# Three half-precision products instead of one fp32 product for the queries of layer 0

## What is computed

```python
x = x + L0_xattn(_layernorm(x), ctx, ctx, Wq, Wk, Wv, Wp)   # 16 heads of 16
#   Q = (q @ Wq), K = (k @ Wk), V = (v @ Wv), causal softmax(Q K^T) V, @ Wp
x = x + L0_ffn(_layernorm(x), router_w, w1, w2)             # 8 experts, the best 2 of each row
#   probs = softmax(xf @ router_w.T); top_k(probs, 2); gelu(xf @ w1) @ w2
x = x + L1_xattn(ctx, ctx, _layernorm(x), ...)
x = x + L1_ffn(_layernorm(x), ...)
```

## Time and profile before

| | before |
|---|---|
| median of three runs | 1009.81 us |
| the profiled execution, its own time | 1009.16 us |
| its span, from the first to the last instruction | 1007.2 us |
| granted TensorE clock, mean over the span | 0.973 |
| busy over the span: TensorE | 918.5 us (91%) |
| TensorE weight loads | 641.0 us (64%) |
| VectorE | 616.9 us (61%) |
| ScalarE | 513.6 us (51%) |
| GpSimd | 423.6 us (42%) |

### The profile page before, as it was taken

The page is one execution under the profiler, slowest core; times in us unless marked ns, Lnnn a source line. Parts: engine busy times, 40 slices in busy tenths (PEclk is TensorE's granted clock), DMA queues, the critical chain, the costliest instruction groups (busy, mean ns, idle before and its releaser), DMA issues. The chain is left out here.

```text
span 1007.2 us, 24069 instructions
## 1 busy us (share of the span) xinstructions
PE 918.5 (91%) x8072; PEld 641.0 (64%) x8072; DVE 616.9 (61%) x1502; ACT 513.6 (51%) x872; POOL 423.6 (42%) x575
## 2 busy tenths in 40 slices
PE   5799999998269999999999999999799999989995
PEld 3555656554136799889899889999544444444552
DVE  4477888875896344445455444565668888545661
ACT  1478888886352433333333333344257667645663
POOL 2487777771201113333433322453256665204550
PEclk9999999999778999999999999999979999999998
DMA  6323444425521111211111111232124221000112
GB/s 190 76 84 93 127 130 130 135 85 168 186 98 53 48 43 43 64 44 43 52 55 43 49 59 54 74 95 75 42 80 108 74 75 48 2 1 17 49 47 59
DMA packets 73729, 75.45 MB, mean 75 GB/s; under 512 B 22730, under 2 KB 66874, under 8 KB 73626
## 3 DMA queue, kind: packets, MB, share of 16 engines
q1 hardware_dynamic: 67146, 56.31, 18.7%
q0 software_dynamic: 6480, 17.70, 6.5%
HBM read 51.64 MB, written 22.34 MB: 73 GB/s over the span
## 5 line engine op out<-in xcount | busy, mean ns | idle before, releaser
L1908 DVE CAST hh_e<-h_e 128x512 f16<-128x512 f32 x128 | 57.9, 452 | 166.4 <-ACT h_e L1787 92.7
L1575 PE MATMUL banks_ea<-experts,hh_e 128*128 x512 | 139.6, 273 | 0.0
L1574 PE MATMUL banks_ea<-experts,hh_e 128*128 x512 | 139.6, 273 | 0.0
L1561 PE MATMUL banks_ea<-xT_e,experts 128*128 128x256 f16 x512 | 139.6, 273 | 0.0
L1576 PE MATMUL banks_ea<-experts,hh_e 128*128 x512 | 139.6, 273 | 0.0
L1562 PE MATMUL banks_ea<-xT_e,experts 128*128 128x256 f16 x512 | 139.6, 273 | 0.0
L1560 PE MATMUL banks_ea<-xT_e,experts 128*128 128x256 f16 x512 | 139.6, 273 | 0.0
L1787 ACT ACTIVATE h_e<-banks_ea 128x512 f32<-128x512 f32 x128 | 76.5, 597 | 85.0 <-PE banks_ea L1562 85.0
L1910 DVE TENSOR_TENSOR hh_e<-h_e,hh_e 128x512 f16<-128x512 f32 x128 | 88.6, 692 | 4.4
L1381 POOL DMA_INDIRECT x_e<-xh_scratch,token x29 | 32.3, 1113 | 135.1 <-PE banks_ea L1501 90.8
L1837 ACT ACTIVATE experts<-banks_ea 77x1024 f32<-77x1024 f32 x64 | 64.9, 1016 | 44.5 <-PE banks_ea L1653 44.5
(11 more groups left out here) (367 smaller groups left out, 2202.7 us busy)
## 6 DMA issues: line engine op xcount, KB each, us to landing
experts<-in_L_ffn_w SPq DMA_DIRECT2D x22, 512.0 KB, 4.3
y_scratch<-y_e SPq DMA_DIRECT2D x32, 256.0 KB, 3.3
x<-in_x SPq DMA_DIRECT2D x32, 128.0 KB, 3.2
experts<-in_x SPq DMA_DIRECT2D x64, 64.0 KB, 2.5
x_scratch<-x SPq DMA_DIRECT2D x16, 256.0 KB, 2.5
xh_scratch<-xn SPq DMA_DIRECT2D x16, 256.0 KB, 2.8
w_late<-in_L_ffn_w SPq DMA_DIRECT2D x8, 512.0 KB, 4.4
w_late<-x_scratch SPq DMA_DIRECT2D x32, 128.0 KB, 2.5
```

Of the source, the lines that this page charges most:

```text
L1561: mm(out, w[0], xT[1][:, c, :], start=False, stop=False)
L1574: mm(out, a[0], w[0], start=m == 0, stop=False)
L1575: mm(out, a[0], w[1], start=False, stop=False)
```

## The change

Wq (with the router's columns) and the transposed rows are split into a high and a low fp16 number each, and q_ps becomes the sum of high x high, high row x low weight and low row x high weight: six fp16 matmuls a tile. ScalarE writes the high half of the rows, VectorE a new `low_rows` behind `maximum(k+2, 0)`. The weights are multiplied by WSCALE = 64 before the split, and the factor is taken out again in the deviation (GpSimd, second operation of an existing instruction) and in the copy of the router's share. TensorE waits for the low half of the rows wherever it waited for `xT`. In `prepare` the fp32 result of `mean` stays in a new `wq`, and two VectorE instructions make the halves.

```diff
@@ prepare, TensorE (wpr)
-                            last = mm(ps[:, 0:E], wpT[:, c, flat(i, P)], G["wq0"][:, c, D:D + E], start=c == 0, stop=c == DC - 1)
+                            last = mm(ps[:, 0:E], wpT[:, c, flat(i, P)], wq[:, c, D:D + E], start=c == 0, stop=c == DC - 1)
@@ prepare, VectorE (mean)
-                        last = nc.vector.tensor_tensor(G["wq0"][:, :, :], wx[:, :, :],
-                                                       ps[:, None, 0:D + E].broadcast_to([P, DC, D + E]), ALU.subtract)
+                        nc.vector.tensor_tensor(wq[:, :, :], wx[:, :, :],
+                                                ps[:, None, 0:D + E].broadcast_to([P, DC, D + E]), ALU.subtract).then_inc(s_high, 1)
+                        dve.wait_ge(s_high, DC + 1)
+                        nc.vector.tensor_scalar(G["wq0"][:, 0, :, :], wq[:, :, :], WSCALE, None, ALU.mult).then_inc(s_high, 1)
+                        dve.wait_ge(s_high, DC + 2)
+                        last = nc.vector.scalar_tensor_tensor(G["wq0"][:, 1, :, :], wq[:, :, :], WSCALE, G["wq0"][:, 0, :, :],
+                                                              ALU.mult, ALU.subtract)
@@ attend_first, GpSimd
-                        nc.gpsimd.tensor_scalar(ve[:, n % 2, :], mv[:, n % 4, 1:2], EPS, None, ALU.add).then_inc(ve_ok, 1)
+                        nc.gpsimd.tensor_scalar(ve[:, n % 2, :], mv[:, n % 4, 1:2], EPS, WSCALE * WSCALE, ALU.add, ALU.mult) \
+                            .then_inc(ve_ok, 1)
@@ attend_first, TensorE: high_transposed, heads_transposed, rows_transposed
-                    after(pe, xT_ok, upto(k + 5))
+                    after(pe, xlo_ok, upto(k + 5))
-                    after(pe, xT_ok, upto(k + 6))
+                    after(pe, xlo_ok, upto(k + 6))
-                    after(pe, xT_ok, f)
+                    after(pe, xlo_ok, f)
@@ attend_first, TensorE: queries
-                    pe.wait_ge(xT_ok, f + 1)
+                    pe.wait_ge(xlo_ok, f + 1)
                     after(pe, lx_ok, f)
                     after(pe, lo_ok, upto(k - 6))
                     for c in range(DC):
-                        last = mm(q_ps[:, 0:D + E], xT[:, f % 2, flat(c, P)], G["wq0"][:, c, :], start=c == 0, stop=c == DC - 1)
+                        for row, weight in ((0, 0), (0, 1), (1, 0)):
+                            last = mm(q_ps[:, 0:D + E], xT[:, f % 2, row, flat(c, P)], G["wq0"][:, weight, c, :],
+                                      start=c == row == weight == 0, stop=c == DC - 1 and row == 1)
@@ attend_first, ScalarE
-                        nc.scalar.activation(xT[:, f % 2, :], t_ps[:, 0:D], ACT.Copy).then_inc(xT_ok, 1)
+                        nc.scalar.activation(xT[:, f % 2, 0, :], t_ps[:, 0:D], ACT.Copy).then_inc(xT_ok, 1)
@@ attend_first, VectorE
-                    nc.vector.tensor_copy(lx[:, f, :], q_ps[:, D:D + E]).then_inc(lx_ok, 1)
+                    nc.vector.tensor_scalar(lx[:, f, :], q_ps[:, D:D + E], 1 / WSCALE, None, ALU.mult).then_inc(lx_ok, 1)
+
+                def low_rows(f):
+                    dve.wait_ge(xT_ok, f + 1)
+                    after(dve, q_done, f - 1)
+                    nc.vector.tensor_tensor(xT[:, f % 2, 1, :], t_ps[:, 0:D], xT[:, f % 2, 0, :], ALU.subtract).then_inc(xlo_ok, 1)
...
                     if tile(k + 2):
                         maximum(k + 2, 0)
+                    if tile(k + 5):
+                        low_rows(k + 5)
                     if tile(k - 6):
                         result(k - 6)
@@ allocate_first
-    G["wq0"], G["v0"] = L.sb("wq0", [P, DC, D + E]), L.sb("v0_sb", [KEYS, B, HEADS, VW])
+    G["wq0"], G["v0"] = L.sb("wq0", [P, 2, DC, D + E], F16), L.sb("v0_sb", [KEYS, B, HEADS, VW])
```

More of the change, by code:

```diff
@@ L188, in prepare @@
         rw = Q.sb("rw", [E, D])
-        wx = Q.sb("wx", [P, DC, D + E])
+        wx, wq = Q.sb("wx", [P, DC, D + E]), Q.sb("wq", [P, DC, D + E])
         mean = Q.sb("mean", [P, P])
@@ L196, in prepare @@
         s_pe, s_act, s_dve, s_v = L.sem("p_pe"), L.sem("p_act"), L.sem("p_dve"), L.sem("p_v")
-        s_k, s_kc, s_wo, s_copies, s_rows, s_mean = (
-            L.sem(f"p_{n}") for n in ("k", "kc", "wo", "copies", "rows", "mean"))
+        s_k, s_kc, s_wo, s_copies, s_high, s_mean = (
+            L.sem(f"p_{n}") for n in ("k", "kc", "wo", "copies", "high", "mean"))
         ident = G["const"][:, CC["ident"][0]:CC["ident"][1]]
@@ L401, in _ @@
                     elif what == "k0":
-                        nc.vector.tensor_copy(k0[:, 0, i, :], ps[:, 0:B * KEYS]).then_inc(s_rows, 1)
-                        dve.wait_ge(s_rows, i + 1)
+                        nc.vector.tensor_copy(k0[:, 0, i, :], ps[:, 0:B * KEYS]).then_inc(s_high, 1)
+                        dve.wait_ge(s_high, i + 1)
                         last = nc.vector.tensor_tensor(k0[:, 1, i, :], ps[:, 0:B * KEYS], k0[:, 0, i, :], ALU.subtract)
@@ L521, in attend_first @@
         xr_in, stored = ([L.sem(f"{n}{i}_0") for i in range(2)] for n in ("xr_in", "stored"))
-        ch, var_ok, rstd_ok, rows_done, xT_ok, q_done, qhi_ok, hi2_ok, qlo_ok, lx_ok, lx_out, lx_in = (
-            L.sem(f"{n}_0") for n in ("ch", "var_ok", "rstd_ok", "rows_done", "xT_ok", "q_done", "qhi_ok", "hi2_ok",
+        ch, var_ok, rstd_ok, rows_done, xT_ok, xlo_ok, q_done, qhi_ok, hi2_ok, qlo_ok, lx_ok, lx_out, lx_in = (
+            L.sem(f"{n}_0") for n in ("ch", "var_ok", "rstd_ok", "rows_done", "xT_ok", "xlo_ok", "q_done", "qhi_ok", "hi2_ok",
                                       "qlo_ok", "lx_ok", "lx_out", "lx_in"))
@@ L1031, in allocate_first @@
     G["latekey"], G["queryid"] = L.sb("latekey", [KEYS, KEYS], BF16), L.sb("queryid", [KEYS, 2, 16, 5], BF16)
-    G["wq0"], G["v0"] = L.sb("wq0", [P, DC, D + E]), L.sb("v0_sb", [KEYS, B, HEADS, VW])
+    G["wq0"], G["v0"] = L.sb("wq0", [P, 2, DC, D + E], F16), L.sb("v0_sb", [KEYS, B, HEADS, VW])
     Q = G["lent"] = Lent(G, LENT_CHUNKS * 2 * HID)
     G["prob"] = Q.sb("prob_0", [KEYS, 2, 2, 2, 512])
-    G["x"], G["xT"] = L.sb("x_0", [P, 8, D]), Q.sb("xT_0", [P, 2, D])
+    G["x"], G["xT"] = L.sb("x_0", [P, 8, D]), Q.sb("xT_0", [P, 2, 2, D], F16)
     G["qhi"], G["qhT"] = Q.sb("qhi_0", [P, 2, D], F16), Q.sb("qhT_0", [P, 2, DC, P], F16)
```

## The result

The changed kernel takes **1011.81 us** (18 runs, 1008.4 to 1016.5) against 1009.93 us of the kernel before in the same measurement (18 runs): a ratio of **1.0025, 95% interval 1.0014 to 1.0037**. Measured twice more, 6 and 12 runs, it gave 1.0054 (1.0039 to 1.0069) and 1.0042 (1.0027 to 1.0057). The profiled execution of the changed kernel took 1011.84 us, with a span of 1010.0 and a mean clock of 0.971.

A forecast was written before the change was run, and what follows sets the result against it. ScalarE's chain, 3.00 us from `heads_transposed` to the scores, was taken as the floor, not TensorE. Preparation +0.95, filling +0.34 and middle -2.01 gave -0.7 us: a median of 1009.1 us, range 1005.5 to 1012.8.

The forecast's parts named there:

- the end of the sum: Whole kernel: 0.95 + 0.34 - 2.01 = -0.7 us, median 1009.1 us; stages after 270 us only shift.
- the one on the slower side: Pipeline steps: `low_rows` takes longer and `heads_transposed` waits in each step, 1017.4 us; chance 0.10.
- The fourth rival: Queries: six fp16 instructions, each with its own weight load, take as long as the four, 1011.5 us; chance 0.07.
- the split: Preparation: two new VectorE instructions, a cast and a subtraction, delay `khi` and all behind it by 0.95 us.
- the filling: Filling of the pipeline: `low_rows` ahead of tile 1's statistics makes GpSimd and ScalarE wait longer, +0.34 us.
- the middle: Steps 5 to 26 of the pipeline: -3.48 + 1.10 + 0.37 = -2.01 us.
- Queries: TensorE's query product of each tile: six fp16 matmuls take 0.68 us, saving 0.29 us a tile.
- ScalarE's floor: Middle of the pipeline: ScalarE's chain holds H to S at 3.00 us, so 22 intervals give up only 3.48 us.
- H to S: In each step, TensorE's time from `heads_transposed` to `scores_by_key` (L689): never below 3.00 us whatever the queries cost.
- VectorE: Middle, even steps: `low_rows` delays the scores, taking back 1.10 us in six long steps and 0.37 in five short ones.
- The wait before `heads_transposed`: Pipeline steps: TensorE's new wait for `low_rows` is covered, by 0.07 us only, and costs nothing.

The follow-up runs named there:

- e4: The changed kernel without `low_rows`, the high rows multiplied a second time instead: 1007.59 us, ratio 0.9984 to the kernel before.
- e15: The changed kernel unaltered, measured a third time: 1014.87 us, ratio 1.0042 to the kernel before.
- e9: The changed kernel with 34 spare matmuls in TensorE's waits of steps 28 to 31: 1010.53 us, ratio 1.0003 to the kernel before.
- e13: The changed kernel with spare matmuls in the filling (20) and in steps 28 to 31 (34): 1008.98 us, ratio 0.9997 to the kernel before.
- e10: e5 with 34 spare matmuls in steps 28 to 31, none in the filling: 1008.85 us, ratio 0.9985 to the kernel before.
- e5: The changed kernel with the weight split behind the second `kc` and, in the filling, statistics ahead of `low_rows`: 1010.78 us, ratio 1.0016 to before.
- e1: The changed kernel unaltered, taken again for a second trace: 1015.03 us, ratio 1.0054 to the kernel before.
- e11: The kernel before unaltered, taken again for a second trace: 1009.89 us, ratio 0.9997 to the kernel before.
- e7: e5 with 54 spare matmuls, in the filling (20) and steps 28 to 31 (34): 1006.80 us, ratio 0.9966 to the kernel before.
- e8: The kernel before with the same spare matmuls as e7, as its control: 1010.47 us, ratio 1.0008 to the kernel before.
- e14: e7 unaltered, measured again: 1006.97 us, ratio 0.9965 to the kernel before.
- e17: The changed kernel with 39 spare matmuls in TensorE's waits of the middle only: 1011.59 us, ratio 1.0015 to the kernel before.
- e16: e4 unaltered, taken again for a second trace: 1006.36 us in its one run.
- e19: e4 unaltered, taken for a third trace: 1009.32 us in its one run.

## Why the prediction was wrong

**The step that failed** is the end of the sum. It has no term for anything behind the last query product, neither for steps 28 to 31 nor for what follows ("The stages after 270 us only shift"), and so assumes in silence that TensorE's clock is granted alike to both kernels. No rival had this mechanism; the one on the slower side that had a chance of 0.10 put the price on `low_rows`. The fourth rival's 1011.5 us is near the 1011.81 of the first measurement by luck: its six products that take as long as four take 0.69 us instead of 0.99. The first measurement lies inside the stated range of 1005.5 to 1012.8, on the other side of before than the forecast; the two later ones, 1015.03 and 1014.87, lie outside.

The schedule came out much as costed. From before to the changed kernel, in steps of the table (without the execution's own half speed at L308): the split +0.79, forecast +0.95, and 0.11 of it comes back by the first rows, so +0.68; the filling +0.60, forecast +0.34; the middle -1.84, forecast -2.01; and +0.18 in the steps behind the last query, which I had at nothing. That is **-0.4 us** where I had -0.7, and a kernel 0.4 us faster cannot be told from no change here.

Term by term:
- *Queries*: 0.69 from start to start, 0.30 saved in this step; forecast 0.29. The Trainium skill (FP8 and Floating Point Precision, TensorE Precision Notes) counts four passes for true FP32, from which 0.74 for three is an estimate; the trace, with 0.69, is a little better.
- *ScalarE's floor*: confirmed by e4, but -2.99 and not -3.48. I let every long interval shrink to 3.00 us. H to S of the 22 intervals in e4: 3.34 became 3.03, and 3.42 became 3.13, its full 0.29 with nothing left over; 3.19 became 3.13 too. The masked steps do not reach the floor.
- *VectorE*: 1.15 taken back, not 1.47. In the long even steps it is 0.09 to 0.24 each, six of them 0.86 in sum (1.10 forecast); in the short ones next to nothing (0.37 forecast), for there the scores come later but S does not: ScalarE's exp still ends last. The wait before `heads_transposed` stayed covered.
- *Split*: the cast took 0.43 (0.40 taken), the subtraction 0.71 (0.70).
- *Filling*: GpSimd's wait for the statistics is 0.90 instead of 0.56, the 0.34 forecast. What I missed is what comes next. Before, its instruction began at 42.22, 0.02 us ahead of VectorE's weight split (L955 at 42.24), and lasted 0.23. Now it begins 0.17 us behind the split and lasts 0.53:

```profile
44.46 0.66 DVE L968 SCALAR_TENSOR_TENSOR experts<-experts 128x512 f16<-128x512 f32 x1
```

```profile
44.63 0.53 POOL L663 TENSOR_SCALAR ve<-mv 128x1 f32<-128x1 f32 x1 [0.90 <-DVE mv L935]
```

**What came in its place** is a fall of the granted clock. Three facts of the runs. The fall to 0.50 near 240 us is in six of eight traces with cheap queries and no spare matmuls, and in none of six with fp32 ones. It costs 1.5 to 1.6 us where it stands (step 28 to the last heads 29.7 instead of 28.18), and 2.9 in e15 (31.07). And kernels with spare matmuls, whose traces lack it, are faster by 2 to 5 us (e9 against the changed kernel), 5.9 us (e13 against e15, on one chip) and 3.1 us (e10 against e5, ratio 0.9985 against 1.0016). That it costs more than its own 1.5 us is visible up to the ranks' product: the six traces with it need 25.6 us on average for that stretch (24.6 to 26.4), the fourteen without 24.5 (23.8 to 25.2); by which path this 1 us is lost was not separated. 1.5 + 1.0 - 0.4 = +2.1 us, against +1.9 in the first measurement; the two others, +5.3 and +5.1, have more in them.

The traces of these two show earlier stretches at 0.50 as well (e1 at 66 to 73 us, 2.2 us in the filling; e15 at 27 to 30, 1.1, and 44 to 51). Between 25 and 80 us nine of the sixteen traces without spare matmuls in the filling have one, that of e11 among them, and none of the four with them (e7, e8, e13, e14); e14 is also 1.9 us faster than e10. How much of the two larger measurements comes from there stays open.

The profiled pair alone would mislead. Its spans differ by +2.8 us: +2.2 by a later start and the half speed of L308, -1.2 by the schedule, +4.1 from step 28 to the ranks' product, +0.2 up to 695 us, and -2.5 behind it, where the change alters nothing.

Why cheap queries bring the fall is argued, and shown only in part. Before, TensorE was busy throughout ahead of its thin last steps; the change makes short waits there, as the 0.33 us of step 12. The thin steps themselves are alike in both kernels, 19.71 and 19.61 us busy of 24. e9 fills their waits, and the fall is gone from its trace, with no run at 0.968 or less. e17 fills the short waits of the middle instead; its trace has no fall either, but the mean clocks of its eleven runs are as low as the changed kernel's. So filling the waits of steps 28 to 31, none longer than 1.77 us, is shown to take the fall away (five traces of five); that the small waits of the middle have a part in it is not shown, though the kernel before has the same thin steps and no fall. The Trainium skill (TensorE: Matmul & The Clock Gate, A second HAM failure mode: psum-queue depth-cycling) describes a clock that swings because of frequent short idles between groups of matmuls; the trace agrees in kind, with one fall of 3.4 us. e4 and e16 had nearly the same waits and no fall, and e19, the same kernel, had it, so it is a matter of odds, and what decides in a single execution stays open.

What the trace of before did show is in the earlier trace rows: the steps behind the last query product idle already, and the change takes busy time away right ahead of them.

## What to carry to other kernels

When a change frees an engine that was busy throughout, ask what its clock will do: a saving behind another engine's floor turns into idle time, and idle time can cost more in clock than the saving was worth. Look for stretches at half clock in several traces of each kernel, and at the mean clock of every run, before arguing with differences of 0.3%. Where TensorE waits for others anyway, spare matmuls can cost nothing (e9) or be in the way (e17); here they turned +0.25% into -0.35% together with two small moves of VectorE's work (e7, e14), and gave the kernel before nothing (e8).

## What the runs showed of the hardware

- The granted clock fell to 0.50 with no wait of TensorE above 1.77 us ahead of it, behind 24 us in which TensorE was 82% busy (19.61 us), and not in every execution of the same kernel (e4 and e16 against e19). In the kernel before TensorE was 82% busy in the same 24 us too (19.71 us), without a fall.
- From the last rows turned for the first layer's experts (L1501, 695.23 us in the trace of before) to the last feed-forward stage (L2253, 910.08 us), in which the change alters nothing, it took 214.85 us in the trace of before, 212.3 in the changed kernel's and 210.6 in e7's. In these three traces the granted clock is at 0.50 there for 10.2 us (near 731), 6.8 us (near 897) and not at all. It moved 4 us between traces, more than the change is worth, here in the changed kernel's favour.
- A GpSimd instruction on one column took 0.23 us when it began just ahead of VectorE's weight split, and 0.53 us when it began 0.17 us into one. In the trace of before, the one at 51.40, inside the split of the earlier trace rows, took 0.66 us.
